# Normalisation of attention probabilities moved to ScalarE, rounding of their transposes moved to VectorE

## The reference, cut to what matters

```python
x = x + 0.5 * ffn(layernorm(x), ...)       # 8 experts, top 2, projection, RMS norm
x = x + attn(layernorm(x), wq, wk, wv, wo, key_weights)
x = x + 0.5 * ffn(layernorm(x), ...)

# attn: 16 query heads, 4 key/value heads, head dimension 128
q = apply_rope(q); k = apply_rope(k)
k = jnp.repeat(k, 4, axis=1) * key_weights[None, :, None, None]
scores = jnp.einsum('bhqd,bhkd->bhqk', q, k) * 128 ** -0.5
scores = jnp.where(causal, -jnp.inf, scores)
attn = jax.nn.softmax(scores, axis=-1)
out = jnp.einsum('bhqk,bhkd->bhqd', attn, v)
return out.transpose(0, 2, 1, 3).reshape(B, S, 2048) @ wo.T
```

## Time and profile before

| | |
|---|---|
| median of three executions | 826.46 us (825.91 to 828.37) |
| the profiled execution | 827.23 us |
| its span (first to last instruction) | 825.4 us |
| mean granted clock of TensorE | 0.989 |
| TensorE busy | 791.6 us, 96% |
| VectorE busy | 655.1 us, 79% |
| ScalarE busy | 507.4 us, 61% |
| GpSimd busy | 517.5 us, 63% |

### The profile page before, as it was taken

One profiled execution on the slowest core, in us unless ns is written; L12 is line 12 of the kernel. 1 busy time (PEld: TensorE's weight loads), 2 busy tenths in 40 slices (PEclk: granted clock), 3 DMA queues, 4 the chain that ended last, 5 costly groups with the idle time before them and its releaser, 6 DMA issues.

```text
span 825.4 us, 16046 instructions
## 1 busy us (share of the span) xinstructions
PE 791.6 (96%) x4712; PEld 697.2 (84%) x4712; DVE 655.1 (79%) x1917; ACT 507.4 (61%) x1250; POOL 517.5 (63%) x408
## 2 busy tenths in 40 slices
PE   7899999869999999999999999999999999999996
PEld 4688887758999989999899998999999988788885
DVE  6888996897678686786876868768687799988876
ACT  3555665657667576676865767557676586344543
POOL 4545739965878778777777777877878761112302
PEclk9999999979999999999999999999999999999998
DMA  9245321201132122212311313122131110000001
GB/s 290 82 144 191 120 85 39 66 13 39 27 77 76 38 51 76 51 27 62 105 28 45 93 30 80 29 85 51 35 92 25 39 27 1 1 1 26 2 26 52
DMA packets 28998, 50.09 MB, mean 61 GB/s; under 512 B 3874, under 2 KB 9634, under 8 KB 28962
## 3 DMA queue, kind: packets, MB, share of 16 engines
q1 hardware_dynamic: 28964, 49.67, 21.5%
HBM read 18.72 MB, written 9.96 MB: 35 GB/s over the span
## 4 chain that ended last, share of the span: by engine, by line
PE 80%; DVE 10%; ACT 3%; issue 2%; POOL 2%; DMA 1%; SPq 1%; POOLq 0%; DVEq 0%; ACTq 0%
PE pt L1713 8%; PE pj L1648 5%; PE pj L1650 5%; PE pj L1649 5%; PE o L1727 5%; PE o L1728 4%; PE o L1729 4%; PE sc L1702 4%; PE sc L1701 4%; PE sc L1700 4%; PE pj L1757 4%; PE pj L1758 3%; PE pj L1759 3%; PE sc L983 3%; PE sc L984 3%; PE sc L985 3%
## 5 line engine op out<-in xcount | busy, mean ns | idle before, releaser
L1273 POOL TENSOR_TENSOR at_ql<-at_rot,at_qh 128x512 fp32r<-128x512 f32 x64 | 82.6, 1291 | 100.5 <-ACT at_qh L1502 100.4
L1549 ACT ACTIVATE at_pth<-pt 128x512 fp32r<-128x512 f32 (+1 forms) x192 | 94.0, 524 | 82.4 <-PE pt L1713 82.4
L1400 DVE TENSOR_TENSOR at_ptl<-pt,at_pth 128x512 fp32r<-128x512 f32 (+1 forms) x192 | 108.9, 594 | 44.9 <-ACT at_pth L1549 44.7
L1543 ACT ACTIVATE at_pr<-at_pr,at_low 128x512 f32<-128x512 f32 (+3 forms) x256 | 140.5, 557 | 4.4 <-DVE at_low L1386 4.2
L1395 DVE TENSOR_SCALAR at_pr<-at_pr,at_inv 128x128 f32<-128x128 f32 (+3 forms) x256 | 107.6, 482 | 2.3
L1285 POOL TENSOR_TENSOR at_rot<-at_rot,gc 128x512 f32<-128x512 f32 x80 | 103.3, 1291 | 6.3
L1281 POOL TENSOR_TENSOR at_rot<-ga,cos 128x512 f32<-128x512 f32 x80 | 103.9, 1298 | 2.4 <-POOL at_ql L1273 2.3
L1283 POOL TENSOR_TENSOR gc<-gc,sin 128x512 f32<-128x512 f32 x80 | 103.7, 1296 | 1.0 <-DMA gc<-ga 1.0
L1713 PE MATMUL pt<-ident,at_pr 128*128 128x128 f32 x640 | 93.5, 277 | 8.3 <-DVE at_ptl L1400 4.6
L1386 DVE CUSTOM_DVE_ANT_0 at_pr<-sc,at_mask 128x512 f32<-128x512 f32 (+2 forms) x192 | 100.7, 548 | 0.2
L1502 ACT ACTIVATE at_qh<-at_rot 128x512 fp32r<-128x512 f32 x64 | 40.6, 634 | 91.1 <-POOL at_rot L1285 91.1
(11 more groups left out here) (286 smaller groups left out, 2265.2 us busy)
## 6 DMA issues: line engine op xcount, KB each, us to landing
gc<-ga SPq DMA_DIRECT2D x160, 128.0 KB, 2.3
ga<-in_attn_w SPq DMA_DIRECT2D x8, 384.0 KB, 4.9
gb<-attn_split SPq DMA_DIRECT2D x6, 512.0 KB, 4.1
at_wo<-attn_split SPq DMA_DIRECT2D x6, 512.0 KB, 4.0
attn_split<-gb SPq DMA_DIRECT2D x6, 384.0 KB, 2.4
attn_split<-gc SPq DMA_DIRECT2D x6, 384.0 KB, 3.3
x<-in_x SPq DMA_DIRECT2D x4, 512.0 KB, 9.5
e_raw<-in_expert_w SPq DMA_DIRECT2D x8, 256.0 KB, 6.6
```

The lines of the kernel that those rows point to most:

```text
L1400: dve.tensor_tensor(ptl[h % 2][:, cols], pt[(NF * h + k) % 2][:, 0:FLEN[k]], pth[h % 2][:, cols].bitcast(F32), ALU.subtract).then_inc(lo_d ...
L1543: act.activation(pr[h % 2][:, cols], pr[h % 2][:, cols], ACT.Exp, bias=low[h % 2][:, i:i + 1], scale=-1.0, accum_out=tot[h % 2][:, i:i + 1 ...
```

## The change

`normalise` goes from VectorE to ScalarE, and `prob_lead` from ScalarE to VectorE. The four reciprocals of a head are made in two halves (`inverse`), the two wide tiles first, each with its own signal. In ScalarE's order `normalise` of n+2 comes after the exponentials and the projection copies and ahead of `rotated_lead` of slot 0 and of `out_lead`. In VectorE's order the copies of fills 0 and 1 come right behind `mask_min`; the copy of fill 2 comes ahead of `out_rest`, and the remainder of fill 2 now behind it. TensorE's, GpSimd's and SP's programs are as they were. The work is still done head by head.

```diff
@@ VectorE
-            def normalise(n, h):
-                dve.wait_ge(ex_done, BT * n + BT)
-                dve.reciprocal(inv[h % 2][:], tot[h % 2][:]).then_inc(inv_done, 1)
-                dve.wait_ge(inv_done, n + 1)
-                for i in range(BT):
-                    a = pr[h % 2][:, OFF[i]:OFF[i] + (i + 1) * P]
-                    dve.tensor_scalar(a, a, inv[h % 2][:, i:i + 1], None, ALU.mult).then_inc(nm_done, 1)
+            def inverse(n, h, half):
+
+                tiles = slice(HT, BT) if half == 0 else slice(0, HT)
+                dve.wait_ge(ex_done, BT * n + HT * half + HT)
+                dve.reciprocal(inv[h % 2][:, tiles], tot[h % 2][:, tiles]).then_inc(inv_done, 1)
+
+            def prob_lead(n, h, k):
+                dve.wait_ge(pt_ready, NF * n + k + 1)
+                cols = slice(FCOL[k], FCOL[k] + FLEN[k])
+                dve.tensor_copy(pth[h % 2][:, cols], pt[(NF * h + k) % 2][:, 0:FLEN[k]]).then_inc(hi_done, 1)
...
                     if more2:
                         mask_min(n + 2, h2)
                     if more1:
+                        prob_lead(n + 1, h1, 0)
+                        prob_lead(n + 1, h1, 1)
+                    if more2:
+                        inverse(n + 2, h2, 0)
+                    if more1:
                         prob_rest(n + 1, h1, 0)
                         prob_rest(n + 1, h1, 1)
+                    if more2:
+                        inverse(n + 2, h2, 1)
...
-                    if more2:
-                        normalise(n + 2, h2)
...
                     if more1:
-                        prob_rest(n + 1, h1, 2)
+                        prob_lead(n + 1, h1, 2)
...
                     out_rest(n, s, h)
+                    if more1:
+                        prob_rest(n + 1, h1, 2)
@@ ScalarE
-            def prob_lead(n, h, k):
-                act.wait_ge(pt_ready, NF * n + k + 1)
-                cols = slice(FCOL[k], FCOL[k] + FLEN[k])
-                act.activation(pth[h % 2][:, cols], pt[(NF * h + k) % 2][:, 0:FLEN[k]], ACT.Copy).then_inc(hi_done, 1)
+            def normalise(n, h):
+                for i in QT:
+                    k = QT.index(i)
+                    if k % HT == 0:
+                        act.wait_ge(inv_done, 2 * n + k // HT + 1)
+                    a = pr[h % 2][:, OFF[i]:OFF[i] + (i + 1) * P]
+                    act.activation(a, a, ACT.Copy, scale=inv[h % 2][:, i:i + 1]).then_inc(nm_done, 1)
...
-                    if more1:
-                        prob_lead(n + 1, h1, 0)
-                        prob_lead(n + 1, h1, 1)
                     if more2:
                         exps(n + 2, h2, QT[:2])
...
                     if h in (1, 2) and ahead:
                         raw_out(s + 1, h + 2)
+                    if more2:
+                        normalise(n + 2, h2)
...
                         rotated_lead(act, s + 1, 1)
-                    if more1:
-                        prob_lead(n + 1, h1, 2)
                     out_lead(n, s, h)
```

More of the change, by code:

```diff
@@ L1477, in vector @@
             scale_rows(last_block, 0)
-            normalise(0, 0)
+            inverse(0, 0, 0)
+            inverse(0, 0, 1)
             mask_min(1, 1)
@@ L1481, in vector @@
             residual_added()
+            prob_lead(0, 0, 0)
+            prob_lead(0, 0, 1)
             prob_rest(0, 0, 0)
@@ L1484, in vector @@
             mean_square(last_block, 1)
-            normalise(1, 1)
+            inverse(1, 1, 0)
+            inverse(1, 1, 1)
+            prob_lead(0, 0, 2)
             prob_rest(0, 0, 2)
@@ L1608, in scalar @@
             raw_out(1, 0)
+            normalise(0, 0)
             rotated_lead(act, 0, 3)
-            prob_lead(0, 0, 0)
-            prob_lead(0, 0, 1)
             step_out(NR)
@@ L1615, in scalar @@
             raw_out(1, 1)
-            prob_lead(0, 0, 2)
+            normalise(1, 1)
             value_lead(0)
```

## The result

| | before | changed |
|---|---|---|
| median | 826.61 us (825.91 to 828.37) | 873.28 us (873.15 to 874.79), four executions |
| ratio, 95% interval | | 1.0565 (1.0545 to 1.0586) |
| span of the profiled execution | 825.4 us | 871.4 us |
| mean granted clock | 0.989 | 0.990 |

The change costs 46.7 us. The forecast was 870.5 within 846 to 892.

A forecast was written before the change was run, and what follows sets the result against it. TensorE alone was taken to bound the loop. Loop +45, first step -4.2, last step +3.5 gave +44 us on a span of 825.4: 869.7, plus 1.8 for the profiled execution, less 0.8 to the median: 870.5, range 846 to 892.

The forecast's parts named there:

- What bounds the kernel: Step loop before the change: bound by TensorE alone, 33.90 us a step; other engines matter only where they come late.
- the bank's spare time: Slot 1 before the change: fill 2's remainder ends 0.64 us before TensorE needs the free transpose bank.
- Costs of the moved work: Per head on ScalarE, normalisation 1.83 us; on VectorE, a queued 512-column copy out of PSUM 0.60 us, so no relief.
- Slot 1: Each of 14 loop steps: normalisation delays rotated key, GpSimd, output copy, then fill 2's remainder; TensorE stalls 2.0 us.
- Slots 2 and 3: Each of 14 loop steps: the ScalarE and VectorE loop exceeds the 6.16 us slot, so each slot stalls 0.62 us.
- The round: Loop between VectorE and ScalarE, one head each time, from fill 2's remainder through normalisation to output remainder: 6.78 us.
- the round gets a second projection copy but TensorE has 2 us more: Slot 3, 8.12 us long: the extra ScalarE copy is covered, so the next slot 0 starts without a wait.
- First step: First step: 9.7 us of waits and clock loss could return, less 5.5 of new waits; 4.2 us saved, bounds 2 and 7.
- Last step: Last step: short slots, a longer round and VectorE's copies and remainders in a row cost +3.5 us, bounds 1 and 6.
- Faster: Rival: the loop keeps its cover, only the first step's gain is left, 822 us; chance 0.1.
- Only slot 1: Rival: only slot 1 stalls, 1.3 us in each of 14 steps, slots 2 and 3 not at all; 842 us, chance 0.1.
- The clock: Rival: slot 1's stall brings a clock fall in each of 14 steps, +24 us more, 894 us; chance 0.08 above 892.

The follow-up runs named there:

- experiment 6: The changed kernel with the four normalising activations scaled by the constant 0.5 instead of the reciprocals: 858.67 us, ratio 1.0390.
- experiment 2: The changed kernel with ScalarE's copy of the rotated key put ahead of the normalisation in slot 0: 851.47 us, ratio 1.0288.
- experiment 8: The changed kernel with only slot 3's two projection copies put ahead of the normalisation on ScalarE: 865.42 us, ratio 1.0457.
- experiment 4: The changed kernel with fill 2's remainder ahead of the output remainder, and rotated key and slot 3's projection copies ahead of the normalisation: 826.30 us, ratio 0.9997.
- experiment 10: As experiment 9, but in the last step ScalarE, not VectorE, copies fills 0 and 1 of the last head: 819.87 us, ratio 0.9926.
- experiment 7: The changed kernel with a head's four reciprocals made at once, behind both wide remainders, instead of in halves: 930.46 us, ratio 1.1260.
- experiment 1: The changed kernel with fill 2's remainder put ahead of the output remainder on VectorE: 860.56 us, ratio 1.0419.
- experiment 9: As experiment 4, plus, in the first step alone, earlier layer norm pieces and fill 0's remainder ahead of fill 1's copy: 822.14 us, ratio 0.9949.

## Why the prediction was right, and where it was off

**What bounds the kernel.** It held. TensorE alone paced the loop; the table by stretch and the bank's spare time of 0.64 us led to the right place.

**Costs of the moved work.** Normalisation 1.81 us against 1.83, the copy 0.60 against 0.60. Taking the row with a pointer rather than the plain copy was right, and experiment 6 shows what the choice was worth: 14.6 us, of them 13.4 in the loop (519.6 to 506.2). That VectorE gets no relief to speak of held too: a copy out of PSUM over 512 columns takes 682 ns on average, the subtraction from the same bank 674.

**Slot 1.** Right in its mechanism (experiment 2 returns it to 6.16 us), 1.73 instead of 2.0 in size. The second rotated copy came 1.3 us later in the step than before, not 1.8 (15.01 us after the step's start against 13.71). The mis-sized term is the time from the key's copy to that copy: 6.43 us before, 6.12 now (394.48 to 400.60 in the changed kernel). I carried GpSimd's pieces over unchanged. Another 0.20 us is ScalarE's: it is done with what stands ahead of the normalisation at 7.08 us of the step instead of 7.28. Of these 0.5 us slot 0, which ends 0.15 earlier, takes a part, the rest of the chain was some 0.1 longer, and 0.27 is left in slot 1. Here are the key's remainder on GpSimd before, and as changed:
```profile
413.95 1.60 POOL L1273 TENSOR_TENSOR at_keys<-at_rot,at_keys 128x512 f32 x1 [1.11 <-ACT at_keys L1502]
```
```profile
395.40 1.29 POOL L1273 TENSOR_TENSOR at_keys<-at_rot,at_keys 128x512 f32 x1 [3.77 <-ACT at_keys L1517]
```

**Slots 2 and 3.** The round is confirmed (6.77 against 6.78) and slot 2 with it (0.56 against 0.62), and so is the round's part of slot 3 (0.59 against 0.62, experiment 8). The step that failed, inside a total that came out right, is slot 3: "the round gets a second projection copy but TensorE has 2 us more". The two copies of the projections stand behind the normalisation in ScalarE's queue, and TensorE's value transposes wait for the first of them: at 421.41 it begins, at 422.04 TensorE goes on. I had looked at whom the copies delay and not at who waits for them. Experiment 8 prices the omission at 0.81 us a step. Other errors hid it in the total: slot 1 was 0.27 too dear, slot 3 was 0.63 too cheap, and slot 0 gained 0.13 that I had not seen. The loop came to 47.6 instead of 45. That the forecast lies within 3 us of the measured time is thus in part luck: the omission alone is 0.81 us in each step, some 11 us, and would have been a larger miss without slot 1's error, slot 0's gain, slot 3's shorter undelayed length and the last step's. (The forecast's last step of arithmetic is 0.2 off: 871.5 less 0.8 is 870.7.)

**First step.** -3.4 instead of -4.2. The sum is near but the experiments say little for its terms: the start of step 1 varied from 197.3 to 203.8 us among the variants of the changed kernel, some of them with the same first step, with the clock's falls in it.

**Last step.** +1.8 instead of +3.5. Experiments 4 and 10 show part of it: +1.8 stays with the loop's order mended (152.96 us from the start of step 15), and 1.2 us of it are the two copies on VectorE.

**The rivals.** *Faster* needed a normalisation of under 0.3 us; it took 1.81. Experiment 4 has a loop without a stall with a normalisation as long, by order alone. *Only slot 1* fell with slots 2 and 3 losing 1.8 us. *The clock* was the nearest of them: stalls of 1.7 us in each of 14 steps left it at 1.00 in every stretch of 100 us from 200 to 700 us, but the slightly longer ones of experiment 7 (listed waits of 1.85 against 1.48 us) did see it fall, in six steps of fourteen. What the rival had wrong as well is the price: there the fall cost the step nothing, because TensorE was no longer the one that set the pace of slot 2.

## What to carry to other kernels

When work moves between engines, price its place in the queue first: list every instruction behind the new place, and for each ask who waits for it, not only how busy the engine is. A few tenths of spare time at a shared bank can hide a chain across three engines, and the same exchange was worth nothing (experiment 4) or +47 us by the order of a few lines; with the first and the last step reordered too it came to -6 us (experiment 10), in part by the clock in the first step. Reorder one link at a time, since a mended one may hand its delay to the next (experiment 1).

## What the runs showed of the hardware

**VectorE's products in SBUF and GpSimd's work took longer side by side, and this cost the kernel before a little in every step.** I had written that the steady steps have little to win, from the 1.28 us of the products in slot 1. In slot 2 of before they took 1.97, beside a GpSimd instruction that was under way when they began. VectorE and GpSimd in the kernel before:
```profile
431.35 1.97 DVE L1395 TENSOR_SCALAR at_pr<-at_pr,at_inv 128x128 f32<-128x128 f32 x4
```
```profile
430.97 1.29 POOL L1285 TENSOR_TENSOR at_rot<-at_rot,gc 128x512 f32<-128x512 f32 x1
```
TensorE in the kernel before, at the start of the transposes that need these products:
```profile
433.30 0.22 PE L1702 MATMUL sc<-at_keys,at_ql 128*128 x1
433.46 0.32 PE L1713 MATMUL pt<-ident,at_pr 128*128 128x128 f32 x1
```
And in experiment 4:
```profile
431.23 0.23 PE L1715 MATMUL sc<-at_keys,at_ql 128*128 x1
431.29 0.40 PE L1726 MATMUL pt<-ident,at_pr 128*128 128x128 f32 x2
```
The gap after the last score is 0.16 us before and 0.06 without the products on VectorE: a loss of 0.1 us that no list of waits showed. In the two slots ahead of it, whose transposes need products of 1.27 and 1.28 us, this gap is 0.06 in the kernel before too (420.96 to 421.02, 427.13 to 427.19). With the order mended, slot 3 is 0.15 and slot 0 is 0.14 us shorter than before, the step 33.6 instead of 33.9 us; this is all that the exchange wins in the loop. Some 0.1 of slot 3's part is seen in these rows, slot 0's part I did not trace. The Trainium skill ("SBUF - State Buffer", "Who interferes with whom") states an exclusive lock on the shared port pair. The traces agree in kind: the products are stretched by 0.69 us, and the key's remainder on GpSimd falls from a mean of 1586 ns before to 1292 in the changed kernel, where they have gone. That the lock is the cause is argued from the overlap in time; no run took GpSimd's instruction away.

**The clock.** In the changed kernel's loop the stall of 1.7 us did not make it fall, in experiment 7 a fall came behind one somewhat longer, but only in the first six steps; why it stopped, behind waits as long, is open. In the first step, where waits of 2 to 4 us follow each other, it fell at different places: the mean from 180 to 190 us was 0.92 in the changed kernel, 0.76 in experiment 4 and 1.00 in experiment 9.
